# A four-stage transformer block on one Trainium2 core: the delta-rule stage unrolled over its batches and woven anew

## What is computed

```python
def _gdn_forward(x, Wq, Wk, Wv, Wa, Wb, Wg, Wo, A_log, dt_bias, conv_q, conv_k, conv_v, o_norm_w):
    beta = jax.nn.sigmoid(x @ Wb) * 2.0
    g = -jnp.exp(A_log)[None, None, :] * jax.nn.softplus(x @ Wa + dt_bias[None, None, :])
    alpha = jnp.exp(g)
    q = _causal_dw_conv_silu(x @ Wq, conv_q).reshape(bsz, seq_len, H, KD)   # 4 taps; H=8, KD=128
    k = _causal_dw_conv_silu(x @ Wk, conv_k).reshape(bsz, seq_len, H, KD)
    v = _causal_dw_conv_silu(x @ Wv, conv_v).reshape(bsz, seq_len, H, VD)   # VD=64
    q = _l2norm(q)
    k = _l2norm(k)
    ...
    def step(state, inp):
        q_t, k_t, v_t, a_t, b_t = inp
        retained = jnp.einsum('bhvk,bhk->bhv', state, k_t)
        ...
        state = a4 * (state - b4 * rk) + b4 * vk
        o_t = jnp.einsum('bhvk,bhk->bhv', state, q_t)
        return (state, o_t)
    ...
    out = out * rms * o_norm_w * jax.nn.silu(gate)
    return out.reshape(bsz, seq_len, VAL_DIM) @ Wo
```

## Time and profile before

| | us |
|---|---|
| median of 3 runs | 3808.57 (3808.51 to 3810.11) |
| the profiled execution | 3808.81 |
| its span, first to last instruction | 3806.2 |
| TensorE busy in the span | 3262.9 (86%) |
| VectorE busy | 2396.6 (63%) |
| ScalarE busy | 1356.5 (36%) |

### The profile page before, as it was taken

How to read it: one execution, slowest core, us unless ns; L and a number is a source line. 1 busy time by engine, 2 the same in 40 slices (tenths; PEclk the granted TensorE clock), 3 DMA queues, 4 the chain that set the end, 5 groups by cost and what they waited for, 6 DMA issues and landing times. The chain is left out here.

```text
span 3806.2 us, 52445 instructions
## 1 busy us (share of the span) xinstructions
PE 3262.9 (86%) x18666; PEld 2525.1 (66%) x18666; DVE 2396.6 (63%) x5801; ACT 1356.5 (36%) x2713; POOL 158.4 (4%) x158
## 2 busy tenths in 40 slices
PE   5999938888999999747989898989898989488887
PEld 2665524445999999714867686868686869355554
DVE  6788425554777777766685858576767673354542
ACT  2333202221444444314534444444444442033232
POOL 0000000015111111000000000000000000000000
PEclk8999958999999999968797988888888886588786
DMA  1000080022899989741011111110111100100000
GB/s 62 23 17 12 11 160 12 11 75 81 305 322 317 320 318 323 253 152 64 34 34 35 34 36 34 35 34 35 34 35 34 35 20 1 53 12 23 12 17 12
DMA packets 203686, 327.31 MB, mean 86 GB/s; under 512 B 37449, under 2 KB 157522, under 8 KB 202258
## 3 DMA queue, kind: packets, MB, share of 16 engines
q1 hardware_dynamic: 196930, 305.94, 24.4%
q0 software_dynamic: 6480, 17.77, 1.2%
HBM read 275.15 MB, written 48.50 MB: 85 GB/s over the span
## 5 line engine op out<-in xcount | busy, mean ns | idle before, releaser
L767 PE MATMUL ex_ps<-ex_xbT,ex_w 128*128 128x128 f32 x4544 | 531.2, 275 | 1.7 <-DMA ex_b<-in_b_all_dram 1.2
L767 PEld LDWEIGHTS ex_ps<-ex_xbT,ex_w 128*128 128x128 f32 x4544 | 524.3, 192 | 6.1 <-DMA ex_b<-in_b_all_dram 1.8
L1378 PE MATMUL de_ps<-de_hT,de_w 128*128 128x512 f32 x640 | 306.2, 636 | 27.6 <-DMA de_w<-in_w_kqv_dram 13.9
L896 ACT ACTIVATE ex_t<-ex_ps,ex_b 128x128 f32<-128x128 f32 x568 | 208.8, 368 | 337.0 <-PE ex_ps L767 319.1
L1378 PEld LDWEIGHTS de_ps<-de_hT,de_w 128*128 128x128 f32 x640 | 129.0, 207 | 188.1 <-issue 186.0
L711 PE MATMUL ex_ps<-ex_xT,ex_w 128*128 128x512 f32 x512 | 230.6, 607 | 12.5 <-DVE ex_gl L1008 9.1
L1008 DVE SCALAR_TENSOR_TENSOR ex_gl<-ex_ps,ex_b,ex_t 128x128 f32<-128x128 f32 (+1 forms) x316 | 123.7, 391 | 137.3 <-ACT ex_t L896 69.4
L711 PEld LDWEIGHTS ex_ps<-ex_xT,ex_w 128*128 128x128 f32 x512 | 98.0, 195 | 131.8 <-issue 115.0
L1735 DVE SCALAR_TENSOR_TENSOR de_ya<-de_kx,de_taps,de_ya 128x512 f32<-128x512 f32 x192 | 142.5, 751 | 49.2 <-ACT de_ya L1574 44.7
L1008 DVE SCALAR_TENSOR_TENSOR ex_gm<-ex_ps,ex_b,ex_t 128x128 f32<-128x128 f32 (+1 forms) x316 | 121.8, 385 | 48.9 <-ACT ex_t L869 46.6
L177 PE MATMUL mx_ps<-mx_hT,mx_w_in 128*128 128x512 f32 x320 | 143.6, 605 | 8.3 <-ACT mx_hT L249 8.3
(11 more groups left out here) (378 smaller groups left out, 6268.3 us busy)
## 6 DMA issues: line engine op xcount, KB each, us to landing
ex_w<-in_w_all_dram SPq DMA_DIRECT2D x144, 1024.0 KB, 6.5
ex_w<-in_w_all_dram SPq DMA_DIRECT2D x72, 512.0 KB, 8.6
de_w<-in_w_kqv_dram SPq DMA_DIRECT2D x80, 256.0 KB, 2.8
de_ab<-alpha_d SPq DMA_DIRECT2D x8, 2048.0 KB, 8.3
ex_xb<-ex_xs_d SPq DMA_DIRECT2D x71, 129.0 KB
ex_xs_d<-ex_blank SPq DMA_DIRECT2D x71, 128.5 KB, 8.3
ex_w<-ex_y_d SPq DMA_DIRECT2D x16, 512.0 KB, 6.1
mx_xin<-in_x_dram SPq DMA_DIRECT2D x8, 512.0 KB, 4.0
```

The costliest lines, as they stand in the source:

```text
L767: m = pe.matmul(ps[:, n % 4, x * BLK:(x + 1) * BLK], w[:, k, part * HID + c * P:part * HID + (c + 1) * P], xbT[sx][:, k, :], start=(k == 0 ...
L896: act.activation(t1[:, n % 2, 0:BLK], ps[:, n % 4, 0:BLK], ACT.Identity, bias=b13[s][:, 0, n:n + 1]).then_inc(t1_ready, 1)
L1378: m = pe.matmul(ps[:, n % 2, :], w[:, g % SLOTS, k, n % 2 * P:(n % 2 + 1) * P], hT[:, k, :], start=(k == 0), stop=(k == KT - 1))
```

## The change

It changes the order of `stage_delta` and little of its arithmetic:

- The loops over the batches are written out; the loop at L1548 and those of the other engines are gone.
- On TensorE the four Gram products stand between chunks 1 and 2 of the recurrence (into banks 0/1 and 6/7, `gram(c)`). `k_transposes` waits for the end of the recurrence's outputs.
- Of the projections only 12 to 17 run ahead of `invert`; 18 and 19 stand between the levels of its first pair of chunks, the four gate projections in its second pair, and so do the transposes and products of `project_out` (through banks 0 and 1).
- The products y6p of the second chunk of a pair and x6p of the first are issued in turn, head by head.
- `kcg` (k scaled by the decays) has one buffer instead of two: `scaled_k(c)` waits for W of the chunk before.
- Xc shares its memory with vb, and GpSimd sets it to zero once per batch; WT has its own; xin shares with o, and x is loaded after the transposes of o.
- On VectorE seven convolutions instead of five stand ahead of the first `decay_u`; the recurrence's steps are spread over the decay scans, the substitution follows at once, and the normalisation of `pb` comes after y5 of the first pair. Its squares are now on ScalarE (`squares`), and the norms of q are prepared at the start of a turn (`query_norm`).

```diff
             def gram_kk(pb, b):
                 pe.wait_ge(s["act"], b * CONV + V0)
+                pe.wait_ge(s["cp"], b * PROJ + V0)
                 if pb is not None:
-                    pe.wait_ge(s["od"], pb * NC + NC)
+                    pe.wait_ge(s["st"], pb * NC + 3)
...
-                        m = pe.matmul(wide(pair(c))[:, hd, :], kc(hd, c), kc(hd, c), start=True, stop=True, skip_group_check=True)
+                        m = pe.matmul(wide(gram(c))[:, hd, :], kc(hd, c), kc(hd, c), start=True, stop=True, skip_group_check=True)
...
             def invert(pb, b):
...
+                    if p:
+                        proj(b, G0, first), proj(b, G0 + 1, first)
+                    else:
+                        proj(b, FILL, first)
...
+                    if p:
+                        proj(b, G0 + 2, first), proj(b, G0 + 3, first)
+                    else:
+                        proj(b, FILL + 1, first)
...
+                    if p and not first:
+                        turn_o(pb, b, 0), turn_o(pb, b, 1)
+                    pe.wait_ge(s["x11"], b * NC + c0 + 1)
+                    for hd in range(H):
+                        m = lower_times_upper(c0, hd)
+                    m.then_inc(s["y6p"], 1)
+                    pe.wait_ge(s["x11"], b * NC + c1 + 1)
+                    pe.wait_ge(s["y6"], b * NC + c0 + 1)
+                    for hd in range(H):
+                        m1 = lower_times_upper(c1, hd)
+                        if hd == H - 1:
+                            m1.then_inc(s["y6p"], 1)
+                        m = times_lower(c0, hd)
+                    m.then_inc(s["x6p"], 1)
+                    if p and not first:
+                        turn_o(pb, b, 2), turn_o(pb, b, 3)
+                    write_w(c0)
+                    pe.wait_ge(s["y6"], b * NC + c1 + 1)
+                    for hd in range(H):
+                        m = times_lower(c1, hd)
+                    m.then_inc(s["x6p"], 1)
+                    if p and not first:
+                        project_out(pb)
+                    write_w(c1)
...
                 def scaled_k(c):
-                    if c >= 2:
-                        act.wait_ge(s["wp"], b * NC + c - 1)
+                    if c:
+                        act.wait_ge(s["wp"], b * NC + c)
...
+                for n in range(Q0, FILL):
+                    cp(n)
+                scaled_k(0)
+                spread_blocks()
+                cp(FILL)
+                x5(0), x5(1)
+                cp(FILL + 1)
+                x11(0), x11(1)
+                step(8, CONV - 1)
+                x6(0)
+                w_out(0)
+                scaled_k(1)
+                x6(1)
+                step(9, CONV - 1), step(10, CONV - 1), step(11, CONV - 1)
+                w_out(1)
...
+                for n in range(7):
+                    conv(n)
+                if not first:
+                    dve.wait_ge(s["cl_ld"], 32 * pb + 32)
+                    decay_state(0), decay_u(0)
+                conv(7)
...
+                y5(0), y5(1)
+                if not first:
+                    normalise()
+                y6(0), y6(1)
+                for n in range(8, 12):
+                    conv(n)
```

## The result

| | us | ratio to before (95% interval) |
|---|---|---|
| before, median | 3809.18 | |
| forecast | 3944 (3850 to 4000) | 1.036 |
| after, median | 4057.45 (4056.39 to 4059.31) | 1.0652 [1.0634, 1.0671] |

The change makes the kernel slower, as forecast, but by 248 us and not by 135, and the time lies outside the range. The span of the profiled execution is 4057.5 us.

A forecast was written before the change was run, and what follows sets the result against it. TensorE was taken as the bound: 86% busy, hardly idling in a middle turn, but not always at full clock. Seven turns of +18 (+126), first body +14 and last -5 on 3808.8 gave 3944 us, range 3850 to 4000.

The forecast's parts named there:

- Head: Start of a middle turn, products of k: written-out loop has no gap, 13.8 us for 18.9, -5.1.
- rival 4: Unrolled lists starve on instruction fetch, each turn paying the old head again: +5 a turn, 3979 us; chance 0.06.
- Recurrence and Gram: Middle turn: 4.7 us gap before the first update, then seven groups at half clock; 61.2 us for 42.8, +18.4.
- To the inverse: Middle turn between v and inverse: fewer projections, 5.3 us idle for Xc behind ScalarE; 25.7 us for 48.4, -22.7.
- First pair: Inverse's first two chunks: two projections come in, waits on ScalarE and VectorE; 43 us for 26.7, +16.3.
- Alternated heads: y6p and x6p in turn in each pair: between 3.5 and 5.3 us, taken as 4.5, some 0.8 gained.
- Second pair: Inverse's last two chunks: gate and output projections partly hidden, waits near 2 us each; 37 us for 26.4, +10.6.
- full clock after y5p: Second pair of the inverse: 36.3 us at full clock after y5p, 39.8 with first half at half clock; 37 taken.
- First body: First batch body: Xc 6.5 us sooner, but six projections in a half-clock inverse; +11 to +20, taken as +14.
- Last body: Last batch body: loses its norm chain and squares, recurrence stays at half clock; -5 us.
- Rivals 1 and 2: Clock survives throughout: -7 a turn, 3759 us, chance 0.10; in recurrence only, or falls late: +8, 3874 us, 0.22.
- rival 3: Clock never recovers in the inverse: pairs 46.9 and 39.8 us, +27 a turn, 4013 us; chance 0.12.

The follow-up runs named there:

- heads apart: Changed kernel with all eight y6p of a pair's second chunk issued before the eight x6p of the first, not alternated by head: 3993.76 us, 1.0486.
- the dummy products alone: Changed kernel plus five unread 128x512 products on TensorE in each middle turn's wait for `decay_u` of chunk 0: 3994.04 us, 1.0489.
- the three mends: Changed kernel with y6p and x6p unalternated, y6 wait moved behind y6p, ScalarE reordered, five unread products before the first update: 3822.39 us, 1.0061.
- the run with the early `u`: Changed kernel with five convolutions instead of seven ahead of VectorE's first `decay_u`, and `u(0)` one step earlier on ScalarE: 4005.1 us, 1.0525.

## Why the prediction fell short

- **Head** (-5.1): as measured, 13.8 us; rival 4 (starving) fell with it.
- **Recurrence and Gram** (+18.4; measured +20.3): right in mechanism and size. The gap was 4.55 for 4.7, then seven groups at half clock. With the gap filled by 4.5 us of work for nobody, 9 us a turn came back, all of it the clock's. Of the missing 1.9 us, 1.6 are the last PQ at half clock behind the gap of 1.55; I had taken the groups there at 1.8. The 1.6 us over in v are of the same origin. So a gap of 1.55 was enough here; the first rows of the inverse, half clock with gaps of 1 to 1.5 us, said so.
- **To the inverse** (-22.7; measured -24.3): the wait for Xc was 5.11 for 5.3, and ScalarE's order is shown as the cause of 2.3 of it.
- **First pair** (+16.3; measured +18.8): the waits came where they were put, 4.50, 2.85 and 1.89 us against 5.0, 2.4 and 2.5 to 4.1, and 1.57 for y6 of chunk 0. The block, 3.6 us over its price, is more than the whole 2.5 us that were missing.
- **Alternated heads** (4.5 us a block; measured 8.1): the step that failed. Its bounds, 3.5 and 5.3, assumed that taking products in turn can't cost. They were the sums with full overlap and with none; a loss by the alternation itself had no bound in the sum and no place among the rivals. The row that should have warned was there: y6p and x6p have weights of two shapes. It is 3.6 us in each of 16 blocks, 58 of the 113 us that the forecast missed; heads apart gave 64 back. The products can overlap, as I had hoped, but only in one shape: then the block took 4.0 us.
- **Second pair** (+10.6; measured +20.9): the largest miss. 3.6 us of the 10.3 are the block. I had the rest at full clock; at half clock and in part, the four gate projections took 5.4 + 3.7 = 9.0 for 6.9, W of chunk 0 3.5 for 1.8, and two transposes of o 1.8 for 1.0: 4.6 us more. So "full clock after y5p" was the second step that failed, some 32 us in seven turns: the clock came back only within the first two projections, and fell again behind the gap of 2.08 us. Some 2 us I can't place.
- **First body** (+14; measured +25): the same block and clock, twice 3.6 of the 11.
- **Last body** (-5; measured -3.9): its recurrence ran at half clock, as forecast, but by another way: the first group is at full clock (1.98 us), and the fall comes behind a gap of 2.00 us for VectorE. The number is in part luck.

Sum of the misses: the seven turns grew by 228.9 us (1539.7 for 1310.8) against 126, so 103; 11 + 1 for the first and last body; 3.4 us for a later start of the stage's first product (0.9 of it a longer wait for weights) less 2.1 elsewhere: 116, all of what the span misses (251 - 135). The turn shown is 14.1 us over its forecast and not 103 / 7 = 14.7, since the turn before that I worked from, 188.0 us, is longer than the mean of the seven, 187.3. Rivals 1 and 2 fell, since chunk 1 ran at 0.50; rival 3 was nearest, with the clock low through most of both pairs, and with the block's measured price it would have come to 4013 + 16 x 3.6 = 4071.

## What to carry over

Look at the shapes of weights before taking small products in turn: different halves of the rows overlap if the shape is one, and each change of shape (here between 128 and 64 columns) costs time, and blocks full of them were followed by half clock. A gap on TensorE ahead of thin products is dearer than its length, and work put in it can pay even if nobody reads it. And read an edit's effect stretch by stretch: a total of +5 us here was +42 in eight bodies, -32 in the ninth and -4 ahead of them.

## What was not expected

- Products of 64x128 in rows 0 to 63 and in rows 64 to 127, in turn: 16 in 1.9 us for 3.7 in one half, at full clock. With 64x64 in turn with 64x128, or with 128x128: 0.62 us a pair for 0.36 to 0.375 apart.
- After such a block with two shapes, without an idle moment, the granted clock fell to 0.50 within it or at its end (three of three), and after the five blocks of one shape or apart it did not. In the kernel it falls without them too: inside the second pair's block with the heads apart (0.61 over it) and with one shape (0.65), both behind a gap of 2.08 us.
- The length of a gap alone doesn't say whether the clock falls. Behind the same 2.30 us ahead of Gram's second half, that half took 5.46 us with the dummy products alone and 3.84, at full clock, with the three mends; the gap of 0.96 us in the kernel before left 1.00 in place, and so did the 1.73 us of the run with the early `u`, for the group behind it, while in the kernel after the clock fell within a group or so of gaps of 1.55, 2.00 and 2.08 us.
- Thin products hold a full clock for 34 us (last body behind six dense products) and don't win it back in 56 us at 0.50. Why the same last body ran at full clock with the alternation ahead of it and at half without stays open.
- Two edits closed a gap with useful work (two convolutions moved back, two projections moved forward), and the gap came back, in part or whole, further on: in one run the same engine, VectorE, was late there, in the other ScalarE.
